# A graph network on one core: edge counts of two window lanes packed into one PSUM word, with smaller units and fewer gathered chunks

## The reference

```python
# layer 1: normalised sum over neighbours
deg  = segment_sum(ones, dst)
norm = rsqrt(deg)[src] * rsqrt(deg)[dst]
x = layernorm(x + segment_sum(x[src] * norm[:, None], dst))
# layer 2: messages whose weights come from a small MLP over each edge's features
h = relu(edge_feat @ W1 + b1); w = (h @ W2 + b2).reshape(e, 4, 8, 8)
m0, m1 = products(x[src], edge_sh, w)
x = layernorm(x + segment_sum(m0 | m1, dst) + x @ si)
```

## Time and profile before

| | |
|---|---|
| runs | 3280.99, 3283.41 and 3286.66 us; median 3283.41 us |
| profiled execution | span from its first to its last instruction 3285.1 us, inside the range of these runs |
| busy over the span | PE 78%, DVE 88%, ACT 39%, POOL 73% |
| layer 1 | starts its tiles at about 78 us; layer 2 issues its first gather at 1171 us |

### The profile page before, as it was taken

How to read it: one execution, slowest core, us unless ns; L and a number is a source line. 1 busy time by engine, 2 the same in 40 slices (tenths; PEclk the granted TensorE clock), 3 DMA queues, 4 the chain that set the end, 5 groups by cost and what they waited for, 6 DMA issues and landing times.

```text
span 3285.1 us, 48226 instructions
## 1 busy us (share of the span) xinstructions
PE 2565.3 (78%) x16782; PEld 1518.9 (46%) x16782; DVE 2879.4 (88%) x5078; ACT 1266.1 (39%) x1963; POOL 2396.7 (73%) x2477
## 2 busy tenths in 40 slices
PE   5788898988888867777777777777777777777776
PEld 4566676666666643333333333333333334333333
DVE  7777887878777749999999999999999999999997
ACT  3788887888888821111111111111111111111111
POOL 1777777777777747777777777777777777777775
PEclk7899999999999978899988988989888888888898
DMA  3111111111111111111111111111111111111112
GB/s 79 45 20 20 20 20 20 20 19 20 20 20 20 30 30 28 28 28 29 31 28 28 29 28 28 28 28 28 29 31 28 28 28 28 29 28 28 29 32 37
DMA packets 169490, 93.10 MB, mean 28 GB/s; under 512 B 112489, under 2 KB 155305, under 8 KB 169129
## 3 DMA queue, kind: packets, MB, share of 16 engines
q0 software_dynamic: 78336, 46.43, 9.5%
q1 hardware_dynamic: 90921, 43.61, 5.4%
HBM read 82.64 MB, written 7.22 MB: 27 GB/s over the span
## 4 chain that ended last, share of the span: by engine, by line
POOL 33%; DVE 27%; PE 16%; issue 15%; ACT 7%; DMA 1%; DVEq 1%; POOLq 0%; SPq 0%; ACTq 0%
POOL gathered L567 33%; DVE stage L1536 9%; PE ps L831 7%; ACT room L636 7%; DVE prod_all L1526 5%; PE ps L846 4%; DVE prod_all L1520 4%; DVE gathered L1206 2%; DVE stage L1510 1%; DVE stage L1506 1%; DVE prod_all L1340 1%; PE ps L771 1%; PE ps L818 1%; PE ps L738 1%; DVE stage L1545 1%
## 5 line engine op out<-in xcount | busy, mean ns | idle before, releaser
L567 POOL DMA_INDIRECT gathered<-x_table,idx x1664 | 1573.2, 945 | 542.1 <-issue 501.3
L636 ACT ACTIVATE room<-ps 128x1089 bf16<-128x1089 f32 x800 | 881.9, 1204 | 177.7 <-PE ps L831 177.3
L567 POOL DMA_INDIRECT gathered<-split_table,efT_all x752 | 770.8, 1025 | 240.1 <-issue 226.4
L952 PE MATMUL ps<-w2t,hT 128*128 128x512 f32 x1664 | 881.6, 656 | 17.8 <-ACT hT L687 17.8
L1536 DVE TENSOR_REDUCE stage<-prod_all 128x192 f32<-128x1536 f32 x416 | 725.7, 1745 | 3.2
L831 PE MATMUL ps<-prod_all,lane 128*128 128x363 bf16 x2640 | 568.6, 325 | 110.1 <-ACT room L636 66.0
L952 PEld LDWEIGHTS ps<-w2t,hT 128*128 128x128 f32 x1664 | 346.0, 214 | 376.6 <-issue 247.0
L687 ACT ACTIVATE hT<-ps,b 128x512 f32<-128x512 f32 x208 | 142.9, 687 | 886.5 <-PE ps L940 886.5
L846 PE MATMUL ps<-stage,room 128*128 128x96 bf16 x7840 | 472.0, 208 | 0.0
L846 PEld LDWEIGHTS ps<-stage,room 128*128 128x128 bf16 x7840 | 426.7, 99 | 81.3 <-issue 3.2
L940 PE MATMUL ps<-efT_all,w 128*128 128x512 f32 x416 | 265.4, 725 | 241.4 <-DMA sh<-in_sh 240.9
(11 more groups left out here) (156 smaller groups left out, 1560.0 us busy)
## 6 DMA issues: line engine op xcount, KB each, us to landing
efT_all<-in_efT SPq DMA_DIRECT2D x104, 256.0 KB
gathered<-x_table,idx POOLq DMA_INDIRECT x1664, 2.4
gathered<-split_table,efT_all POOLq DMA_INDIRECT x752
sh<-in_sh SPq DMA_DIRECT2D x104, 32.0 KB
split_table<-stage SPq DMA_DIRECT2D x1, 2352.0 KB, 7.3
idx<-in_src SPq DMA_DIRECT2D x104, 8.0 KB, 1.6
scaled_x_table<-room SPq DMA_DIRECT2D x2, 784.0 KB, 3.4
x_table<-x_sb SPq DMA_DIRECT2D x7, 224.0 KB, 4.5
```

Of the source, the lines that this page charges most:

```text
L567: pool.indirect_dma_start(to, None, table, bass.IndirectOffsetOnAxis(ap=at, axis=0)).then_inc(landed, 16)
L636: act.activation(counts[u % 2][:, :, t * TWIN:(t + 1) * TWIN].rearrange("p (r h) w -> p r h w", r=RANGES), ps_ring[i % 2].rearrange("p r ( ...
L952: mm = pe.matmul(ps_bank[j % 2][v], hT[j // 2][:, t * P:(t + 1) * P], w2t[:].rearrange("p h c o i -> p (h c o i)"), start=False, stop=True)
```

## The change

Two window lanes share one word. The window now has 12 places as 2 x 6 (`HALF`). A new tensor `side` holds for each edge 1/256 where its place is in the first half, and 256 where it is in the second. The spread key is built over 98 x 6 lanes, and the compare is followed by a multiplication with `side` in the same instruction. So a PSUM word holds the count of a place in the first half divided by 256, plus that of the place six further times 256. ACT multiplies with 256 while copying and writes int32: the low 16 bits hold one count and the high 16 bits the other. PE reads the room as float16, in which such a small integer is a number of 2^-24 times the integer; `take_rows` multiplies with 2^24.

With it come: two count matmuls of 294 columns per tile in place of three of 363; a PSUM ring of three slots of two banks; units of ten tiles (10 x 12 = 120 columns); all evictions by ACT; eight spread-key buffers; `key`, `low` and `side` in float16; and three gathered chunks per pattern in place of five, which makes 39 gathered chunks and 104 units. The diff, cut to what matters:

```diff
-UT = 11
+UT = 10
+HALF = 6
+SIDE = 256.0
+COUNT_SCALE = 2.0 ** 24
...
-DVE_TILES = (5,)
-CPP = 5
+CPP = 3
...
-RANGES = 3
-HR = 33
+RANGES = 2
+HR = 49
+RING = 3
...
-KR = 5
+KR = 8
...
-    RW = HR * TWIN
-    LW = -(-RANGES * RW // 4) * 4
+    RW = HR * HALF
+    LW = RANGES * RW
...
-        key = sb("key", [P, DT])
-        low = sb("low", [P, DT])
+        key = sb("key", [P, DT], F16)
+        low = sb("low", [P, DT], F16)
+        side = sb("side", [P, DT], F16)
...
-        counts = [t[:].bitcast(BF16).rearrange("p (h w) -> p h w", w=P) for t in room]
+        counts = [t[:].bitcast(F16).rearrange("p (h w) -> p h w", w=P) for t in room]
+        count_words = [t[:].bitcast(I32).rearrange("p (h w) -> p h w", w=P // 2) for t in room]
...
-        ps_ring = [ps[:, RANGES * b:RANGES * (b + 1), 0:RW] for b in range(2)]
+        ps_ring = [ps[:, RANGES * b:RANGES * (b + 1), 0:RW] for b in range(RING)]
...
-                act.activation(counts[u % 2][:, :, t * TWIN:(t + 1) * TWIN].rearrange("p (r h) w -> p r h w", r=RANGES),
-                               ps_ring[i % 2].rearrange("p r (h w) -> p r h w", w=TWIN),
-                               ACT.Copy).then_inc(s_evict, 1)
+                act.activation(count_words[u % 2][:, :, t * HALF:(t + 1) * HALF].rearrange("p (r h) w -> p r h w", r=RANGES),
+                               ps_ring[i % RING].rearrange("p r (h w) -> p r h w", w=HALF),
+                               ACT.Copy, scale=SIDE).then_inc(s_evict, 1)
...
-                act.activation(rows_u[:], ps_dense, ACT.Copy).then_inc(s_dsb, 1)
+                act.activation(rows_u[:], ps_dense, ACT.Copy, scale=COUNT_SCALE).then_inc(s_dsb, 1)
...
-                    if t not in DVE_TILES:
-                        evict(u, t)
+                    evict(u, t)
...
-                if i >= 2:
-                    if (i - 2) % UT in DVE_TILES:
-                        pe.wait_ge(s_evict_d, dve_evicts(i - 1))
-                    else:
-                        pe.wait_ge(s_evict, act_evicts(i - 1))
+                if i >= RING:
+                    pe.wait_ge(s_evict, i - RING + 1)
...
+            for to, offset in zip(counted_places(side), counted_tiles(rel_tile)):
+                dve.tensor_scalar(to, offset, HALF - 0.5, None, ALU.is_ge).then_inc(s_side, 1)
+            dve.wait_ge(s_side, 2)
+            for to, of, offset in zip(counted_places(key), counted_places(side), counted_tiles(rel_tile)):
+                dve.scalar_tensor_tensor(out=to, in0=of, scalar=-float(HALF), in1=offset, op0=ALU.mult,
+                                         op1=ALU.add).then_inc(s_side, 1)
+            dve.wait_ge(s_side, 4)
+            dve.tensor_scalar(side[:], side[:], SIDE - 1.0 / SIDE, 1.0 / SIDE, ALU.mult, ALU.add).then_inc(s_side, 1)
...
-            for to, of, offset in zip(counted_places(key), counted_places(high), counted_tiles(rel_tile)):
-                dve.scalar_tensor_tensor(out=to, in0=of, scalar=float(TWIN), in1=offset, op0=ALU.mult,
-                                         op1=ALU.add).then_inc(s_key, 1)
+            dve.wait_ge(s_side, 5)
+            dve.scalar_tensor_tensor(out=key[:], in0=high, scalar=float(HALF), in1=key[:], op0=ALU.mult,
+                                     op1=ALU.add).then_inc(s_key, 1)
...
-                dve.tensor_scalar(spread[i % KR], near_lanes[:], key[:, i:i + 1], None, ALU.is_equal).then_inc(s_spread, 1)
+                dve.tensor_scalar(spread[i % KR], near_lanes[:, 0:LW], key[:, i:i + 1], side[:, i:i + 1], ALU.is_equal,
+                                  ALU.mult).then_inc(s_spread, 1)
...
-                        made = u * UT + t - (KR - 1)
-                        if 0 <= made < DT and made % UT in DVE_TILES:
-                            evict(made // UT, made % UT)
```

More of the change, by code:

```diff
@@ L82, in gnn_program @@
     assert CHUNKS % 2 == 0 and CHUNKS >= 8 and n_out + UW <= SUMW and NP % SPLITS == 0
[L83 to L90, removed]
+    assert NP % HB == 0 and NP == RANGES * HR and RW <= WIDE and LW % 4 == 0 and CHUNKS % 4 == 0 and NP % GB == 0
+    assert CG * TPC + DT == TILES and CG % 2 == 1 and UT * 2 * HALF <= P and TWIN <= 2 * HALF and DT % TPC == 0 and NP * TWIN <= 2048
     def chunk_tile(n):
@@ L258, in gnn_program @@
         wide_oh = [prod[0].rearrange("p t b i o -> p (t b i o)")[:, 0:2 * WIDE].rearrange("p (t w) -> p t w", t=2)] * 2
-        key = sb("key", [P, DT])
-        low = sb("low", [P, DT])
-        dst_c = key
+        key = sb("key", [P, DT], F16)
+        low = sb("low", [P, DT], F16)
+        side = sb("side", [P, DT], F16)
+        dst_c = room[0][:, NC * D:NC * D + DT]
         high = oh_all[1][:].rearrange("p t w -> p (t w)")[:, 0:DT]
@@ L347, in gnn_program @@
         s_key = sem("s_key")
+        s_side = sem("s_side")
         s_member = sem("s_member")
@@ L824, in count_tile @@
                 pe.wait_ge(s_spread, i + 1)
-                if i >= 2:
-                    if (i - 2) % UT in DVE_TILES:
-                        pe.wait_ge(s_evict_d, dve_evicts(i - 1))
-                    else:
-                        pe.wait_ge(s_evict, act_evicts(i - 1))
+                if i >= RING:
+                    pe.wait_ge(s_evict, i - RING + 1)
                 for r in range(RANGES):
-                    mm = pe.matmul(ps_ring[i % 2][:, r, :], ohlow[:, i % LR, 0:P], spread[i % KR][:, r * RW:(r + 1) * RW],
+                    mm = pe.matmul(ps_ring[i % RING][:, r, :], ohlow[:, i % LR, 0:P], spread[i % KR][:, r * RW:(r + 1) * RW],
                                    start=True, stop=True)
@@ L889, in _ @@
             with pe.Else():
-                pe.wait_ge(s_key, 7)
+                pe.wait_ge(s_key, 6)
                 pe.wait_ge(s_pos, 1)
@@ L1026, in _ @@
             dve.tensor_copy(near_lanes[:, 0:WIDE], lane_f[:]).then_inc(s_dve_c, 1)
-            dve.tensor_scalar(near_lanes[:, WIDE:2 * WIDE], lane_f[:], float(WIDE), None, ALU.add).then_inc(s_dve_c, 1)
-            dve.tensor_scalar(near_lanes[:, 2 * WIDE:LW], lane_f[:, 0:LW - 2 * WIDE], 2.0 * WIDE, None,
-                              ALU.add).then_inc(s_dve_c, 1)
+            dve.tensor_scalar(near_lanes[:, WIDE:LW], lane_f[:, 0:LW - WIDE], float(WIDE), None, ALU.add).then_inc(s_dve_c, 1)
             dve.tensor_copy(low_lanes[:, :, 0:43], lane_f[:, 0:P + 1].rearrange("p (a b) -> p a b", b=43)).then_inc(s_dve_c, 1)
-            steps[0] += 4
+            steps[0] += 3
             slope = z_row[:].rearrange("p g f -> p (g f)")[:, 0:CHUNKS]
@@ L1388, in clear_pads @@
             def clear_pads(k):
-                dve.memset(counts[k][:, :, UT * TWIN:P], 0.0).then_inc(s_pads, 1)
+                dve.memset(count_words[k][:, :, UT * HALF:P // 2], 0).then_inc(s_pads, 1)
             def join_parts(n):
@@ L1424, in _ @@
                 dve.sem_inc(s_wmm[layer], 1)
-            dve.wait_ge(s_key, 7)
+            dve.wait_ge(s_key, 6)
             dve.wait_ge(s_pos, 1)
```

38 lines of the change are left out of this document (15 added, 23 removed).

## The result

The changed kernel takes 3047.07 us (median of 4 runs, 3046.46 to 3048.86) against 3285.03 us of the kernel before on the same chip (4 runs, three of them in the table ahead of the prediction): ratio 0.927, 95% interval 0.926 to 0.929. The profiled execution has a span of 3047.0 us, 238.1 under the 3285.1 of before. The forecast was 3078 us.

What follows compares the result with a forecast made beforehand. GpSimd's gathers were taken to bound layer 1. Fewer gathers -215, waits +8 and start +1.5 sum to -205.5 us against 3285.1: 3079.6, as a median 3078 us; range 3045 to 3185, by itself 3055 to 3110.

Steps and rivals of the forecast that it cites:

- What bounds: Layer 1: GpSimd's gathers stay the bound, 8.06 us per unit against TensorE's 7.85; 160 fewer gathers give -215.1 us.
- The sign that I read in the earlier trace: Layer 1: GpSimd waits for TensorE never longer than 0.3 us, while TensorE waits for gathered rows up to 8.4 us.
- The units: TensorE's work per group of tiles whose counts are applied together: 7.55 us plus 0.3 of boundary stall, 7.85 us.
- rival 1: Units bind layer 1, not gathers: 8.8 us per unit, -139 us, 3145 us in all; chance 0.18.
- the far end of rival 1: Float16 counts load more slowly on TensorE: 1.6 us more per unit, 9.5 us, 3217 us in all.
- The waits between near-equal chains: Layer 1: GpSimd and TensorE, close to each other, lose 1% of the stage, +8 us (bounds 0 and 30).
- that tail: From layer 1's last gather to layer 2: taken as fixed, GpSimd standing 28.87 us until layer 1's rows are written.
- The price of one gather: Layer 1: a gather's 85 ns over 0.94 us, blamed on VectorE instructions, stays; 0 us taken (-9 to +13).
- Rival 2: Gathers get dearer: VectorE's instructions hold each 0.17 us more, +103 us over 608 gathers, 3181 us; chance 0.10.
- The instruction that the prediction set beside the lock: At the start: VectorE instruction from 81.27 to 84.70, behind which a gather lasting 3.77 us ended by 1.16 us.
- Rival 3: VectorE's two-operation compare runs one element per step: spread key 0.68 us, +69 us, 3352 us; chance 0.12.
- The start: Five new VectorE instructions ahead of the first reading of the branch flag: +1.5 us (0 to 3).

Runs made afterwards that it cites:

- run 12: Changed kernel with two PSUM count buffers in place of three, and lane numbers for a window's one-hots read from the freed PSUM bank: 3038.5 us.
- Runs 1 to 3: Kernel before, unpacked, with 39 chunks and ten-tile units: 3373.9 us; changed kernel with 29 chunks, 120 units: 3118.8 us; with 44 chunks, 96 units: 3160.4 us.
- runs 5 to 9: Changed kernel, one-hots in four pieces over four tiles: 3096.2 us; six key buffers and keys of 588, 896, 960, 1024 lanes: 3051.1, 3216.5, 3252.5, 3309.5 us.
- runs 11 and 12: Changed kernel with two PSUM count buffers in place of three: 3059.4 us; the same with one-hot lane numbers read from PSUM: 3038.5 us.
- run 5: Changed kernel with a gathered window's one-hots in four instructions, each behind one of four tiles: 3096.2 us.

## Why the prediction was right, and where it was off

*What bounds.* Right, and as narrow as forecast: POOL stays the bound, and the 160 gathers are the gain. The sign that I read in the earlier trace rows was half of the evidence; PE's waits for rows are the other half, 18.3 us in the changed kernel, and in run 12, where they are gone, the units bind. At 1.353 us per step those gathers are 216.5 us where I had 215.1. Runs 1 to 3 show the condition: unpacked units bind at 39 chunks, packed ones do at 29.

*The units.* Two placings of the changed kernel without a window between them, and two with one, on PE's timeline:

```profile
397.16 0.42 PE L851 MATMUL ps<-place_u,rows_u 128*96 128x104 f32 x2
404.18 0.42 PE L851 MATMUL ps<-place_u,rows_u 128*96 128x104 f32 x2
...
412.00 0.42 PE L851 MATMUL ps<-place_u,rows_u 128*96 128x104 f32 x2
```

7.02 us without a window, 7.82 with one. I had 7.55 and 0.3 of stall on average; rival 1 (8.8 us per unit) is out. Float16 counts load as fast as bfloat16 did: 98 ns by the group above (99 before), and the chain that ended last has 65 applies in 2.76 us, 42.5 ns each, so the far end of rival 1 is out too:

```profile
911.92 2.76 PE ps L840 x65
```

ScalarE's int32 copy takes 670 ns (I had 730).

*The waits between near-equal chains.* I took +8 us. They did not come: POOL's step holds no wait for PE over 0.3 us, and the tail behind the last gather became 6.6 us shorter. I had called that tail fixed and put no term for it; it is not, as run 12 shows too, where it grows by 11.6 us over its control.

*The price of one gather.* This is the term that was mis-sized, and it fell outside its own bounds: I took 0 (-9 to +13), and the step shrank by 0.027 us, -16.8. My upper estimate let the 85 ns of hold grow with VectorE's share of busy time, the lower one with the length of the instruction that is met. The second had the right sign. By the timelines of before, the 644 gathers that met VectorE at work but no one-hots of a window were held 28 us in all, 203 of them by over 0.02 us; after, 500 such gathers were held 6 us, 22 of them by over 0.02. What stays is the window's one-hots: 26 of the 32 us that 592 gathers are held in all. Rival 2 (dearer gathers) did not occur, but runs 5 to 9 show that its price was no fancy: a key of 1024 lanes brings +0.41 us per gather.

Why the one-hots hold is settled by runs 11 and 12: it is the second input from SBUF, not the 1.41 us. The instruction that the prediction set beside the lock is of that kind as well, two inputs in SBUF. The Trainium skill (SBUF — State Buffer, section "Who interferes with whom") says that a VectorE instruction with two SBUF inputs contends with GpSimd instructions that read SBUF, and that one with at most one SBUF input, outside the two-port modes, does not; this agrees. It infers, for DMAs in general, that such a two-input instruction leaves GpSimd's descriptor generation alone; for these gathers, whose row numbers lie in SBUF, the runs show the contrary: they end 0.83 us behind the instruction.

Left open is why 588 lanes hold hardly anything and 896 hold a gather by 0.34 us on average, while the 1092 of before held it by less. In the changed kernel it is mostly VectorE that gives way, as on the timelines of POOL and VectorE:

```profile
401.33 0.94 POOL L566 DMA_INDIRECT gathered<-split_table,efT_all  x1 [0.30 <-issue]
```
```profile
401.80 0.61 DVE L1341 TENSOR_SCALAR prod_all<-near_lanes,key,side 128x588 bf16<-128x588 f16 x1
```

The usual key takes 0.42 us. Of the 206 keys that began 0.42 to 0.60 us after the start of a gather that was not held, 203 were lengthened by over 0.06 us, 36 us in all, and each of them ended 1.08 or 1.09 us after that start; of the other keys none was. So the phase in which a key meets a gather decides whether VectorE gives way there. With 1024 lanes only 7 keys were lengthened, and the gathers were held instead. Two pairs with one key lengthened by 0.19 us take 1.26 us and a gather's step 1.25, which may keep the two in step at 588 lanes; no run tested that. In the kernel before VectorE rested for 126 us for want of a free key buffer. Why some gathers are held through eight pairs and more, no run told apart; it happened twice at 588 lanes even in run 12, 3.7 us each.

*VectorE's second operation.* Rival 3 is out: a pair steps by 0.54 us, 0.34 of it the spread key, where I had 0.30 and the rival 0.68, on VectorE's timeline:

```profile
80.62 0.29 DVE L1339 TENSOR_SCALAR lane<-low_lanes,low 128x129 bf16<-128x129 f16 x1 [0.20 <-DVE pos L1163]
80.82 0.43 DVE L1341 TENSOR_SCALAR prod_all<-near_lanes,key,side 128x588 bf16<-128x588 f16 x1
81.16 0.28 DVE L1339 TENSOR_SCALAR lane<-low_lanes,low 128x129 bf16<-128x129 f16 x1
```

The key's mean of 454 ns, not the 390 expected, contains the waits just named. The fast rate holds with two operations, 0.25 ns per lane between 588 and 1024; the rule of the Trainium skill (VectorE: DVE Perf Modes, section "Mode 4×_2P — both tricks at once") weighed in rival 3 agrees with it.

*The start.* 2.6 us later, where I had 1.5 (0 to 3).

Together: -1.4 (gather step), -16.8 (price), -8 (waits that did not come), -6.6 (tail) and +1.1 (start) are -31.7 us, and the forecast was 31 us too high.

So 3047 lies under the 3055 to 3110 that I gave the forecast by itself. It lies inside the full range by 2 us, and that was luck: the lower end of 3045 was put down to cheap gathers, no loss and a start that costs nothing, but the bounds of these three terms give 3078 - 9 - 8 - 1.5 = 3059.5. The 14 us below that stood for no term; a gather price below its bound and the shorter tail came in their place.

## What to carry to other kernels

When an engine that issues gathers is the bound, look not only at how many it issues but at what VectorE runs beside them: here the three lengths that VectorE's keys were stretched to cost about twice their own time, and one operand moved from SBUF to PSUM was worth 21 us, until the units bound. Mean durations of the bound engine's instruction, by the kind of neighbour that they met, show where to look before any experiment does. That the issuing engine never waits does not yet make it the bound: look at who waits for what it fetches. And when work is shifted between two engines that are close to each other, run the neighbours of the chosen split: both were slower here, by 72 and 113 us.

## What was not expected of the hardware

- A gather begun inside a VectorE instruction with two SBUF inputs ended 0.83 us behind it, nearly a whole gather later, even where VectorE then rested; beside one of the same shape and length with one input in PSUM it lasted 0.94 us.
- Four such instructions of a quarter the length, back to back, held gathers nearly as long as one (986 against 994 ns on average); set apart they brought holds of 3 to 4 us beside the pairs between them (1073 ns on average).
- Gathers were held for up to 4.1 us beside instructions of 0.42 us and less (run 5), and for up to 6.5 us beside keys of 1024 lanes, 0.53 us each.
- A key that began 0.42 to 0.60 us after the start of a gather that was not held was lengthened and ended 1.08 or 1.09 us after that start, 203 times out of 206 in the changed kernel.
